# Layer 0's banded self-attention: float32 tiles of 32 rows kept on the chip, maxima from blocks of 64 queries by 128 keys

## The reference

```python
D_MODEL = 256; N_HEADS = 16; D_HEAD = 16; WINDOW = 64
attend = (j <= i) & (j >= i - window_size)          # query i, key j
mask = jnp.where(attend, 0.0, -1e9)
Q, K, V = (split_heads(x @ W.T) for W in (Wq, Wk, Wv))
scores = jnp.einsum('bhqd,bhkd->bhqk', Q, K) / sqrt(16) + mask
weights = jax.nn.softmax(scores, axis=-1)
out = jnp.einsum('bhqk,bhkd->bhqd', weights, V)
return merge_heads(out) @ Wo.T
```

## Time and profile before

| what | us |
| --- | --- |
| median of three runs (2614.08, 2615.79, 2620.44) | 2615.79 |
| the profiled execution | 2614.69 |
| span of its trace | 2613.0 |
| layer 0's attention, first to last instruction of its own | 22.7 to about 281 |
| of it, before the first exponential's scores | 22.7 to 67.6 |
| the sixteen groups | 67.5 to 272.5 |
| the tail after them | 272.5 to 282.4 |

### The profile page before, as it was taken

One profiled execution on the slowest core, in us unless ns is written; L12 is line 12 of the kernel. 1 busy time (PEld: TensorE's weight loads), 2 busy tenths in 40 slices (PEclk: granted clock), 3 DMA queues, 4 the chain that ended last, 5 costly groups with the idle time before them and its releaser, 6 DMA issues. The chain is left out here.

```text
span 2613.0 us, 28449 instructions
## 1 busy us (share of the span) xinstructions
PE 2086.1 (80%) x10279; PEld 1314.2 (50%) x10309; DVE 1706.7 (65%) x2551; ACT 1189.9 (46%) x1889; POOL 588.5 (23%) x346
## 2 busy tenths in 40 slices
PE   5789889695689997969875788888788989283895
PEld 3456557584323324857732444444475654161574
DVE  5555455423677755732177999999965766858675
ACT  2334422110266673511046899999943236412340
POOL 3331122120242212012100675565301210000100
PEclk8889999698799998969988899999989989696896
DMA  6554220343655500034310000000031000000001
GB/s 127 87 87 46 71 97 1 107 155 117 107 73 73 65 1 22 1 110 147 119 59 38 0 1 1 1 1 1 33 102 37 1 0 1 0 8 22 1 1 39
DMA packets 108550, 127.88 MB, mean 49 GB/s; under 512 B 15591, under 2 KB 99444, under 8 KB 107381
## 3 DMA queue, kind: packets, MB, share of 16 engines
q1 hardware_dynamic: 100118, 113.45, 18.8%
q0 software_dynamic: 2880, 7.48, 0.8%
q10 hardware_dynamic: 5408, 5.07, 0.6%
HBM read 92.29 MB, written 33.29 MB: 48 GB/s over the span
## 5 line engine op out<-in xcount | busy, mean ns | idle before, releaser
L3360 DVE TENSOR_TENSOR_SCAN l2s_h<-l2w_aw 128x2048 f32<-128x2048 f32 x64 | 290.1, 4533 | 5.0 <-ACT l2s_rs L3483 5.0
L3288 PE MATMUL l2s_big<-g_xn,g_ident 128*128 128x512 f32 x512 | 258.5, 607 | 11.4 <-ACT g_xn L3476 6.3
L3447 POOL TENSOR_SCALAR l2w_aw<-l2w_aw 128x2048 f32<-128x2048 f32 x64 | 212.2, 3316 | 141.5 <-DVE l2w_aw L3352 136.3
L591 DVE TENSOR_REDUCE l1at_nm<-l1at_s 128x1 f32<-128x512 f32 x256 | 161.9, 683 | 67.6 <-PE l1at_s L441 66.6
L3280 PE MATMUL l2s_c_ps<-g_ident,l2s_h 128*128 128x128 f32 x1024 | 148.9, 279 | 55.8 <-ACT g_xn L3476 36.8
L3280 PEld LDWEIGHTS l2s_c_ps<-g_ident,l2s_h 128*128 128x128 f32 x1024 | 117.2, 142 | 146.5 <-issue 86.9
L691 ACT ACTIVATE g_xn<-l1at_s 128x512 f32<-128x512 f32 x256 | 143.6, 598 | 84.5 <-PE l1at_s L465 83.9
L3476 ACT ACTIVATE g_xn<-l2s_c_ps,l2s_ct 128x512 f32<-128x512 f32 x256 | 162.5, 686 | 16.0 <-PE l2s_c_ps L3280 15.6
L591 DVE TENSOR_REDUCE l0at_nm<-l0at_s 128x2 f32<-128x384 f32 x128 | 69.7, 556 | 90.0 <-PE l0at_s L441 88.9
L3469 ACT ACTIVATE l2w_aw<-l2s_dt,l2w_A 128x2048 f32<-128x2048 f32 x64 | 128.2, 2004 | 0.0
L3288 PEld LDWEIGHTS l2s_big<-g_xn,g_ident 128*128 128x128 f32 x512 | 82.0, 190 | 81.7 <-ACT g_xn L3476 59.1
(11 more groups left out here) (873 smaller groups left out, 4811.9 us busy)
## 6 DMA issues: line engine op xcount, KB each, us to landing
l1f_w<-in_L_ffn_w_dram SPq DMA_DIRECT2D x16, 1024.0 KB, 6.5
l0f_w<-L_ffn_experts_inter_dram SPq DMA_DIRECT2D x7, 1024.0 KB, 5.3
l0f_w<-n_L_ffn_experts_out_dram SPq DMA_DIRECT2D x7, 1024.0 KB, 9.7
l0at_qs<-l0at_parts SPq DMA_DIRECT2D x18, 256.0 KB, 9.1
l0at_ks<-l0at_parts SPq DMA_DIRECT2D x18, 256.0 KB, 17.9
l1at_qs<-l1at_parts SPq DMA_DIRECT2D x18, 256.0 KB, 9.1
l1at_ks<-l1at_parts SPq DMA_DIRECT2D x18, 256.0 KB, 20.8
expert_rows<-g_zeros SPq DMA_DIRECT2D x1, 4096.0 KB, 12.8
```

Of the source, the lines that this page charges most:

```text
L591: V.tensor_reduce(nm[:, s % 2, qts[0]:qts[-1] + 1, r], s1[:, u % 3, 0:len(qts) * KEYS].rearrange("p (q k) -> p q k", k=KEYS), AX, ALU.max, ...
L3288: nc.tensor.matmul(acc[:, tb, :], ident[:], hCT[:, tb, :], start=n == 0, stop=n == NST - 1).then_inc(acc_done, 1)
L3360: V.tensor_tensor_scan(out=h_all[:, i % 2].rearrange("p c t -> p (c t)"), data0=dA[:, i % 2].rearrange("p c t -> p (c t)"), data1=wd[:, i ...
L3447: nc.gpsimd.tensor_scalar(wd[:, i % 3], wd[:, i % 3], 10.0, -10.0, ALU.min, ALU.max).then_inc(clipped, 1)
```

## The change

The call in the program becomes `banded_attention(nc, "l0at", ...)`, a new function. Layer 1's attention keeps the old one.

- Q and K stay float32 and stay on the chip. ACT takes each projected chunk out twice, once for the even heads and once for the odd heads (L1145), with a scale per partition that zeroes the other heads, so that `qz` and `kz` hold each head as a tile of 32 rows in SBUF. The other 16 rows of a tile carry a one in `kz` and, later, the negated maximum in `qz`. The splits, the trips to DRAM, `pick`, and the bfloat16 masks are gone.
- A group is now four heads of equal parity, one in each block of 32 rows. `max_scores` (L945) is four matmuls per unit, each 32 rows by 64 queries by 128 keys: two query tiles, and in each the lower and upper half into PSUM partitions 0 to 63 and 64 to 127. There is no mask matmul.
- DVE takes the maximum with `tensor_tensor_reduce` (L1081) on 128 columns: PSUM plus mask, times minus one, minimum. There are two per unit, and each is two instructions in the stream.
- The maxima lie in `nmx`, 128 columns per query tile. PE turns them in float32 (L953) and DVE adds the result straight to `qz` (L1088); the copy by ACT and the spreading by POOL are gone.
- `prob_scores` (L966) is two matmuls per unit, 32 rows by 128 keys by 192 queries (128 for the last key tile), without a mask. After the exponential (L1153) POOL sets what lies outside the band to zero with two `affine_select` per unit (L1215, L1217), and `weigh` (L983) waits for that instead of the exponential.
- The maxima run 14 units ahead (`LEAD`), and the second half of batch 0's projections and its values are put between the first units of maxima (`EARLY`).

The diff's core:

```diff
-            self_attention(nc, "l0at", c, of("L0_attn_"), given=False, window=True)
+            banded_attention(nc, "l0at", c, of("L0_attn_"))
...
+    def max_unit(m):
+        s, i = m // NU, m % NU
+        return s, (i + 2 - LEAD) % GH, (2 * (i // GH), 2 * (i // GH) + 1)
+    def prob_unit(u):
+        s, i = u // NU, u % NU
+        return s, i % GH, (2 * (i // GH), 2 * (i // GH) + 1)
...
+                    rows = slice(HP * r, HP * (r + 1))
+                    for v, q in enumerate(qts):
+                        for half in range(2):
+                            q0 = q * P + half * BAND
+                            k0 = max(q0 - BAND, 0)
+                            ins = nc.tensor.matmul(s1[half * BAND:(half + 1) * BAND, m % 3, v * P:(v + 1) * P], qz[rows, b % 2, o, e, q0:q0 + BAND],
+                                                   kz[rows, b % 2, o, e, k0:k0 + P], start=True, stop=True)
+                    ins.then_inc(s1_ready, 1)
...
+                    for v, kt in enumerate(kts):
+                        q0, n = columns(kt)
+                        ins = nc.tensor.matmul(s2[:, u % 2, v * SPAN:v * SPAN + n], kz[rows, b % 2, o, e, kt * P:(kt + 1) * P],
+                                               qz[rows, b % 2, o, e, q0:q0 + n], start=True, stop=True)
+                    ins.then_inc(s2_ready, 1)
...
+                def weigh(w):
+                    s = w // NW
+                    b, o, e = place_of(s)
+                    pe.wait_ge(cut_done, (w + 1) * GH)
...
+                    for v, q in enumerate(qts):
+                        to = nmx[:, s % 2, q, col:col + 1]
+                        ins = V.tensor_tensor_reduce(masked[:, m % 3, v], s1[:, m % 3, v * P:(v + 1) * P], mask[:, 1 if q else 0, :], -1.0, 3e38,
+                                                     ALU.add, ALU.min, to)
+                    ins.then_inc(s1_free, 1)
...
+                    for e in range(2):
+                        bias = top[:, 1 - e:2 - e] if n else 0.0
+                        ins = E.activation((qz, kz)[n][:, b % 2, o, e, :], m_ps[:, at, :], ACT.Identity, bias=bias, scale=own[:, n, e:e + 1])
+                    ins.then_inc(bank.free, 1)
...
+                    Chain(pool, cut_step, u).step(G.affine_select(out=near, in_=near, compare_op=ALU.is_ge, fill=0.0, base=0, pattern=[[0, 2], [1, P]],
+                                                                  channel_multiplier=-1))
+                    G.affine_select(out=far, in_=far, compare_op=ALU.is_ge, fill=0.0, base=0, pattern=[[0, 2], [-1, P]],
+                                    channel_multiplier=1).then_inc(cut_done, 1)
```

316 lines of the change are left out of this document (added).

## The result

The change made the kernel slower: 2805.88 us against 2615.79, a ratio of 1.0727 with a 95% interval of 1.0699 to 1.0755. One further run of the kernel before took 4577.18 us and is left out of its median. The forecast was 2593 us, and the range ended at 2665. The profiled execution of the changed kernel has a span of 2802.4 us, 189.4 more than before.

A forecast was written before the change was run, and what follows sets the result against it. It took PE, with holes, to bound the groups and a chain through DRAM the prelude. Prelude -23.5, groups 0 and tail +1.5 on 2614.7 gave 2593 us; the range was 2570 to 2665.

The forecast's parts named there:

- Prelude: Before the groups: without splits and DRAM wait, first probability unit at about 44 instead of 67.58, 23.5 us earlier.
- DVE's price: Groups: two maxima per unit at 0.295 + 0.13 us each make 0.85 us, taken as the unit's bound.
- ACT's loop: Groups: two PSUM buffers shared by matmul, exponential and semaphores bound a unit at 0.70 us.
- The overlap: Score units: maxima and probabilities of unequal shape on other rows run together, PE's share about 0.64 us per unit.
- The rival: Score units: unequal shapes exclude each other and drain PE, 1.36 us per unit, 2647 us; chance 0.35.
- three signs of being wrong: Probabilities starting later than 50 us, a unit over 1 us, or the stage's clock under 0.8.
- The clock: Groups: clock falls to half on narrow tiles, 22.2 us per group, about 2745 us; chance 0.08 together with POOL.
- The sum of the groups: Sixteen groups: 8 x 0.85 + 6.0 = 12.8 us each, 205 us in all, no difference from before.
- Full-width work: Groups: full-array matmuls (weigh, turns, projections, values, outputs) on PE take 6.0 us per group.
- POOL and the tail: POOL's cut, 8.8 us in a 12.8 us group, is covered; a last cut and weigh add 1.5 us.
- the drained case at full clock: Score units: the shapes exclude each other, 1.36 us per unit; 2647 us, or 2665 with 0.14 more per unit; chance 0.35.

The follow-up runs named there:

- e5_pairs: Changed kernel with PE's order made two units of probabilities, then two units of maxima, instead of one and one; 2593.81 us, ratio 0.9923.
- e9_after_same_rows: Changed kernel with its maxima on the same 32 rows as the probabilities beside them; 2814.08 us, ratio 1.0753.
- e1_rows128: Changed kernel with both score matmuls contracting over all 128 rows instead of 32, exponential scale zero; 2640.89 us, ratio 1.0076.
- e2_one_shape: Changed kernel with the maxima in the probabilities' tile shape, two matmuls per unit instead of four, 192 columns; 2578.07 us, ratio 0.9837.

## Why the prediction was wrong, step by step

**Prelude, right in size by luck.** 44.45 us against about 44. Its inside was not as told: the maxima did not go at DVE's pace. From the first maximum to the first probability unit are 15.7 us, and the sum had 15.1; but DVE's 14 units take only 14 x 0.42 = 5.9 of them, where the sum had 11.9. PE's projections and values between the maxima set the pace, one of them at half clock (3.65 us for L918 at 30.25). Two errors of opposite sign met. The timeline of the prelude, all engines:

```profile
28.74 0.29 DVE L1081 CUSTOM_DVE_ANT_0 l0at_masked<-l0at_s,l0at_mask 128x128 f32<-128x128 f32 x1 [4.19 <-PE l0at_s L945]
...
29.32 0.29 DVE L1081 CUSTOM_DVE_ANT_0 l0at_masked<-l0at_s,l0at_mask 128x128 f32<-128x128 f32 x1
29.53 0.08 DVE L1081 DVE_READ_ACCUMULATOR2_ANT l0at_nmx<- 128x1 f32 x1
29.53 0.29 DVE L1081 CUSTOM_DVE_ANT_0 l0at_masked<-l0at_s,l0at_mask 128x128 f32<-128x128 f32 x1
...
30.25 3.65 PE L918 MATMUL l0at_m_ps<-g_xnT,l0at_wqk 128*128 128x512 f32 x4
```

**DVE's price, mis-sized by two.** One maximum follows the other after 0.21 us (29.32 to 29.53), so a unit is 0.42 us and not 0.85. The records of neighbours overlap (0.29 + 0.08 us in 0.21), and the sum added durations where it should have added distances between starts. With the shapes overlapping, the next bound of the sum was ACT's loop at 0.70. No run shows it as the limit: in e5_pairs a unit is 0.75, but PE waits for ACT for only 2.3 us there, and ACT for PE for 111.

**The overlap, the step that failed.** "If the two shapes overlap as well" was taken for the likeliest from a row in which tiles of equal shape overlap, against rows 8 and 9, where every change of shape waits. Those rows could not tell whether tiles on other rows escape it; e9_after_same_rows shows that they do not. The rival had the price right: 1.36 us per unit forecast, 1.37 measured at full clock, with 0.20 and 0.15 us lost where 0.20 and 0.146 were forecast; and 2647 us forecast for drains at full clock, 2641 measured in e1_rows128. Two of the three signs of being wrong that the prediction named came: a unit over 1 us, and a clock under 0.8.

**The clock, a rival that was priced alone.** It stood at 0.08 together with POOL, and with the narrow tiles overlapping. But a drained unit and half a clock came together: by the prediction's own terms 8 x 1.36 + 6.0 = 16.9 us per group at full clock become 33.8 at half, and no line of its list had both. The row given beside it was the stretch on 64x64 tiles at clock 1.00. There fourteen records of 0.213 us of columns stand in 1.73 us, so two tiles of 64 rows by 64 run at a time; in the changed kernel it is one of 32 rows by 128, or two of 32 by 64, half as much. The stretch at 0.50 with PE always busy is no narrow tile either:

```profile
L1940 PE MATMUL l0fr_lg_ps<-l0fr_wg,g_xnT x64: 221/361/382, 475.5 to 493.5; 128*128 128x8 f32 x64
```

Its weights are 128 by 128 and 8 columns move. It shows that a PE that never waits can stand at half clock, and not what tiles of 32 rows do.

**The sum of the groups.** Full-width work was put at 6.0 us per group. In e1_rows128 a unit is 1.33 us on average; (244.7 - 128 x 1.33 + 14 x 0.59) / 16 = 5.2 us. That term was 0.8 too high, some 13 us in all.

**POOL and the tail.** The cut is nearly hidden, as told. The tail was to grow by 1.5 us; with the start of the next stage it grew by 5.3. It runs partly at half clock too (L1011 with sixteen records takes 5.52 us there, L510 before took 3.69); how much of the 5.3 us that is was not taken apart.

**The range** ended at 2665, above the drained case at full clock. The measured 2805.88 lies 141 us beyond it; drained units at half clock had no place in the list.

## What to carry to other kernels

Here matmuls on small tiles gained from standing beside each other only when they had one shape. So choose the shapes of neighbouring matmuls together, even where one of them gets more columns, or put equal ones next to each other in PE's list. A PE that is busy all the time can still run at half its clock: read the granted clock beside the busy share, and when a narrow tile will run with nothing beside it, price the half clock too. When two rivals can come true together, price them together.

## What the runs showed of the hardware

- Taking turns between 32*128 and 32*64 tiles costs 0.20 us of each probability unit and 0.15 us of each maxima unit at full clock, and as much when the two share no row (changed kernel) as when they share theirs (e9_after_same_rows).
- PE starts matmuls of one shape on other row blocks 0.01 us apart and ahead of their place in the list: the second unit's L964 at 123.39 stands in the list behind the second pass of the first (123.63), e2_one_shape.
- With 32-row score tiles mostly one at a time the clock in the groups was 0.57 to 0.65 although PE waited for 1 us or so; with one of the two shapes on 128 rows, in the same order and with nearly the same pitches (and a scale of zero in the exponential), it was 0.99.
- The maximum on DVE is two instructions of 0.29 and 0.08 us, but one maximum of 128 columns starts 0.21 us after the other.
